# Layer-0 attention: row maxima turned by DVE in 32x32 blocks, a third bank for scores, the turned output in the bank of the values

## Chip, cores, metric

The kernel runs on 1 core of one Trainium2 chip. The metric is the device time of one execution in microseconds (us). A shorter time is better. The engines are PE (matmul), DVE (vector), ACT (scalar), POOL and SP, which here only issues DMAs.

## What is computed

Two transformer layers on x of 4 x 512 x 256 fp32, each with a modulation of its own. The change lies in the attention of layer 0, whose 16 query heads of width 16 share one key and one value head:

```python
q = x @ Wq.T                          # 16 heads of 16
kv = x @ Wkv.T
k, v = jnp.split(kv, 2, axis=-1)      # one head of 16
attn = jnp.einsum('bhqd,bkd->bhqk', q, k) / math.sqrt(HEAD_DIM)
attn = jnp.where(causal, attn, -1e9)
attn = softmax(attn, axis=-1)
out = jnp.einsum('bhqk,bkd->bhqd', attn, v)
return out.reshape(bs, seq, 256) @ Wo.T
```

Around it, `x = x + ga * attention(layernorm(x) * (1 + ca) + sa)`, and then a router with 64 experts (the best 8, an expert bias only) in the same form. Layer 1 has attention with 16 heads of 128 and a gated feed-forward part; the change doesn't touch it.

## The kernel before

The work of layer 0's attention is a loop of 44 steps for each of the 4 batches (`steps0`, written out on each engine). A batch has 4 groups (NG) of 4 heads, and a group 11 units (GU): one or more heads with a tile of 128 queries and the 512, 384, 256 or 128 keys that the causal mask leaves. Each engine runs the same steps, and at each step it does, in the order of the code, its part of several units that are at different stages. The stage of a unit is set by a lag in steps:

- **Scores**, lag 0. PE multiplies q by k (L1204, bf16 parts, 96 rows), adds the mask (L1206) into bank 0 or 1, by the parity of the step, and DVE takes the negated maximum of each row (L912, `negmax`). PE waits at step n for the reduction of step n-2 (`max0`), and at the first step of a batch for all reductions of the batch before.
- **Maxima to rows**, once a group, one group (11 steps) later. DVE splits the 16 maxima of each query into two bf16 parts (L923, L924, tile `nmp`). One step later PE turns the 128x32 tile into 32x128 (L1178, bank 4), ACT copies it (L656, tile `nmt`), and SP issues two DMAs (L429) that lay it as two rows under q in `qst`, so that the next product subtracts the maximum by itself.
- **Turned scores**, lag TURN = 17. PE multiplies k by q with the two extra rows (L1189) and adds the turned mask (L1191) into bank 2 or 3, and ACT takes the exponential into `probs` or `pT` (L664). The first unit of a group waits for the two DMAs (`nm_ready`).
- **Values**, lag VALUE = 19. At four of 11 steps PE multiplies by v (L1215) into bank 5, which holds a whole group. ACT copies it one step later (L672, `oRaw`); one step after that PE turns it (L1224) into bank 4, and DVE divides by the sums there (L930, L934, `oTok`). The next group's first values wait for the copy (`o_copied`), and the next turn of maxima for the reading of bank 4 (`oev0`).
- **After attention**, lag AFTER = 22 behind the batch: `after0(n)` spreads the output projection (n = 3 on PE, which waits for `oL` of DVE), the residual, the norm, the router, the expert bias and the next norm over 44 more steps.

SP's queue goes by a fixed order: for each group first the reload of q for the next batch (6 DMAs of 64 KB, L421, once the turned scores of the group are done), then the DMAs of maxima of a later group.

The program's order is written by hand; nothing is reordered. All engines wait on counting semaphores.

## Time and profile before

| | us |
|---|---|
| median of 3 runs | 1459.1 (1458.41 to 1460.87) |
| profiled execution, its own time | 1461.47 |
| its span, first to last instruction | 1459.7 |
| busy: PE, DVE, ACT, POOL | 1270.8, 1043.7, 678.6, 542.2 |
| mean granted clock of PE | 0.93 of full |

The busy times are of the whole span; layer 0's attention with what follows it runs from 110 us to 464 us. A time in a row of the timeline is counted from the span's start. In brackets stands how long the engine had waited before and what ended the wait. Of matmuls, a row's length includes the time in the array, so lengths of neighbours overlap, and the distance between starts is what one costs. "PEld" is PE's port for weights, which runs beside the matmuls.

### The profile page before, as it was taken

To read this page: it belongs to the slowest core of one execution; us is meant where nothing else is said; L and a number is where in the kernel's file an instruction comes from. 1 tells how busy PE (TensorE), PEld (TensorE's weight loads), DVE (VectorE), ACT (ScalarE), POOL (GpSimd) and SP (SyncE) were. 2 spreads that over 40 slices of the span, in tenths; PEclk is the share of its full clock that TensorE was granted. 3 is DMA by queue.
4 is the path that set the end of the run, shared out by engine and by line. 5 is a ranking of instruction groups with operands and counts; after the bars stand their busy time and mean duration, and the time that the engine had idled before them with its cause. 6 is when DMAs were issued, how large, how long until landed. Compare 5 with 4: busy or idle time off the path is not lost.

```text
span 1459.7 us, 25278 instructions
## 1 busy us (share of the span) xinstructions
PE 1270.8 (87%) x7740; PEld 956.4 (66%) x7740; DVE 1043.7 (71%) x3041; ACT 678.6 (46%) x1605; POOL 542.2 (37%) x496
## 2 busy tenths in 40 slices
PE   5898887776844899999899999999999899996998
PEld 3553443344443677777677778777788688785887
DVE  5766768777657876877876877876777766674773
ACT  2334534343403645545645545645655645652332
POOL 0000000000000988889888889888721300000000
PEclk8898989888856999999999999999999999998999
DMA  5121100101111010210110210110200200000000
GB/s 167 43 66 35 32 23 27 44 20 37 40 48 62 30 39 11 96 38 0 39 39 10 95 36 4 33 36 8 91 32 19 70 29 7 22 0 0 15 14 29
DMA packets 29850, 54.31 MB, mean 37 GB/s; under 512 B 5664, under 2 KB 21872, under 8 KB 29280
## 3 DMA queue, kind: packets, MB, share of 16 engines
q1 hardware_dynamic: 26544, 42.93, 8.9%
q0 software_dynamic: 2096, 6.51, 1.4%
q10 hardware_dynamic: 1152, 4.19, 0.7%
q8 instruction: 23, 0.38, 0.1%
q14 instruction: 35, 0.29, 0.1%
HBM read 41.86 MB, written 11.63 MB: 37 GB/s over the span
## 4 chain that ended last, share of the span: by engine, by line
PE 53%; DVE 34%; issue 10%; ACT 3%; DVEq 0%; DMA 0%; ACTq 0%; SPq 0%
PE bank L1307 10%; PE bank L1285 7%; PE bank L263 6%; PE bank L264 6%; PE bank L265 6%; DVE qkst L977 4%; DVE negmax L912 4%; PE bank L1296 4%; DVE qk L996 4%; PE bank L1074 3%; PE bank L1275 3%; PE bank L1204 2%; PE bank L1189 2%; PE bank L332 2%; DVE negmax L1009 1%
## 5 line engine op out<-in xcount | busy, mean ns | idle before, releaser
L528 POOL TENSOR_SCALAR gtmp<-gidx,lut 128x344 f32<-128x344 int32 (+2 forms) x210 | 301.5, 1436 | 21.3
L531 POOL TENSOR_TENSOR gacc<-gacc,gtmp 128x344 f32<-128x344 f32 (+2 forms) x210 | 183.4, 873 | 17.5
L1285 PE MATMUL bank<-kT,qT 128*128 128x128 f32 (+3 forms) x512 | 179.8, 442 | 9.2 <-ACT probs L720 9.1
L521 POOL DMA_DIRECT2D gidx<-in_idx_gate x4 | 2.2, 543 | 465.3 <-DMA h_saved<-wft 465.3
L1307 PE MATMUL bank<-pT,v 128*128 128x128 f32 x1280 | 155.4, 277 | 12.2 <-ACT pT L713 12.2
L912 DVE TENSOR_REDUCE negmax<-bank 128x1 f32<-128x512 f32 (+3 forms) x176 | 109.8, 639 | 74.3 <-PE bank L1206 73.3
L1009 DVE TENSOR_REDUCE negmax<-bank 128x1 f32<-128x128 f32 (+3 forms) x256 | 123.4, 484 | 54.6 <-PE bank L1286 53.4
L720 ACT ACTIVATE probs<-bank,negmax 128x128 f32<-128x128 f32 (+3 forms) x256 | 135.6, 530 | 49.9 <-DVE negmax L1009 47.3
L1307 PEld LDWEIGHTS bank<-pT,v 128*128 128x128 f32 x1280 | 148.0, 192 | 15.9 <-DVE oL L1019 15.9
L977 DVE BATCH_NORM_STATS2 qkst<-qk 128x6 f32<-128x128 f32 x512 | 110.0, 279 | 63.4 <-issue 63.4
L263 PE MATMUL bank<-wgH,hL 128*128 128x512 f32 x384 | 153.6, 400 | 0.1
L264 PE MATMUL bank<-wgL,hH 128*128 128x512 f32 x384 | 152.1, 396 | 0.0
L265 PE MATMUL bank<-wgH,hH 128*128 128x512 f32 x384 | 152.0, 396 | 0.0
L713 ACT ACTIVATE pT<-bank 128x128 f32<-128x128 f32 (+3 forms) x256 | 111.0, 437 | 52.0 <-PE bank L1296 51.7
L1004 DVE TENSOR_SCALAR probs<-probs,rsum 128x128 f32<-128x128 f32 (+3 forms) x256 | 123.7, 483 | 7.9
L699 ACT ACTIVATE qk<-bank 128x512 f32<-128x512 f32 x128 | 76.4, 598 | 99.5 <-PE bank L265 98.8
L1296 PE MATMUL bank<-identf,probs 128*128 128x128 f32 x640 | 112.8, 278 | 10.8 <-DVE probs L1004 7.4
L1296 PEld LDWEIGHTS bank<-identf,probs 128*128 128x128 f32 x640 | 70.0, 141 | 58.6 <-issue 28.8
L996 DVE TENSOR_TENSOR qk<-qk,sm 128x512 f32<-128x512 f32 x128 | 98.1, 835 | 0.5
L1019 DVE TENSOR_TENSOR oL<-bank,oH 128x512 fp32r<-128x512 f32 x64 | 44.1, 689 | 75.5 <-ACT oH L727 75.3
L664 ACT ACTIVATE pT<-bank 128x384 f32<-128x384 f32 (+1 forms) x112 | 58.9, 537 | 84.0 <-PE bank L1191 77.2
L1204 PE MATMUL bank<-kst,qst 96*128 96x512 bf16 (+3 forms) x256 | 73.0, 339 | 19.7 <-DVE negmax L912 18.7
(191 smaller groups left out, 2809.0 us busy)
## 6 DMA issues: line engine op xcount, KB each, us to landing
hH<-h_saved SPq DMA_DIRECT2D x16, 512.0 KB, 4.0
hL<-h_saved SPq DMA_DIRECT2D x16, 512.0 KB, 4.7
qst<-q_parts SPq DMA_DIRECT2D x96, 64.0 KB, 2.3
wg<-in_wqkv SPq DMA_DIRECT2D x4, 1536.0 KB, 8.3
wo<-in_wo SPq DMA_DIRECT2D x4, 512.0 KB, 9.2
out<-x SPq DMA_DIRECT2D x8, 256.0 KB, 2.1
x<-in_x SPq DMA_DIRECT2D x1, 1536.0 KB, 10.0
wmod<-in_wmod SPq DMA_DIRECT2D x1, 1536.0 KB, 11.9
```

Of the source, the lines that this page charges most:

```text
L263: pe.matmul(o, wL, mH, start=start, stop=False)
L264: pe.matmul(o, wH, mL, start=False, stop=False)
L265: return pe.matmul(o, wH, mH, start=False, stop=stop)
L528: link(pool.tensor_scalar(tmp if j else acc, part, float(j), lut1[0:rows, j:j + 1], ALU.is_equal, ALU.mult))
L531: link(pool.tensor_tensor(acc, acc, tmp, ALU.add))
L912: dve.tensor_reduce(negmax[:, at:at + (heads - 1) * QT + 1:QT], bank[n % 2][:, 0:heads * w].rearrange("p (h k) -> p h k", h=heads), AX.X, ...
L977: last = dve.bn_stats(qkst[:, u * HG + h, :], qk[:, u // 2, u % 2, h * HD1:(h + 1) * HD1])
L996: dve.tensor_tensor(rows, rows, r.to_broadcast([P, HG, HD1]), ALU.mult).then_inc(qk_norm, 1)
L1009: dve.tensor_reduce(negmax[:, i:i + 1], bank[SCORE_BANKS[i % 3]][:, 0:n], AX.X, ALU.max, negate=True).then_inc(max1, 1)
L1285: pe.matmul(bank[SCORE_BANKS[i % 3]][:, 0:n], qT[:, h, t * P:n], kT[:, h, 0:n], start=True, stop=False)
L1296: last = pe.transpose(bank[5 + i % 2][:, k * P:(k + 1) * P], probs[:, i % 4, k * P:(k + 1) * P], identf[:, :])
L1307: last = pe.matmul(bank[7][:, t * P:(t + 1) * P], v1[:, k, h * HD1:(h + 1) * HD1], pT1[:, h % 2, at:at + P], start=(k == 0), stop=(k == t))
```

## The change

1. The matmul that turned the maxima and ACT's copy are gone. DVE, after the split, transposes the 128x32 tile in four blocks of 32x32 (`dve.transpose`, tile `nmt` is now 128x32), after a further wait for the subtraction. Four DMAs instead of two bring it into the same two rows of `qst`, each with 32 queries of the 16 items: 2x16 pieces of 64 B, where two DMAs had 16 pieces of 256 B each. Before writing `nmt` DVE waits for the DMAs of the group before.
2. Bank 4, freed, is a third bank of scores: PE waits at step n for the reduction of step n-3 (also over the border of a batch).
3. The turned output goes into bank 5, where the values were. The next group's first values now wait for the reading of it (`oev0`).
4. TURN is 16 and not 17; VALUE and AFTER follow, 18 and 21.

```diff
-TURN = 17
+TURN = 16
+S_BANKS = (0, 1, 4)
...
-        nmt = sb(s0, "nmt", [NMP * ITEMS, P], BF16)
+        nmt = sb(s0, "nmt", [P, NMP * ITEMS], BF16)
...
-                sp.wait_ge(nm_copied, b * NG + g + 1)
-                for j in range(NMP):
-                    sp.dma_start(qst[SHIFT + j:SHIFT + j + 1, g * HG * SEQ:(g + 1) * HG * SEQ].rearrange(
-                        "p (i q) -> p i q", q=P), nmt[j * ITEMS:(j + 1) * ITEMS, :]).then_inc(nm_ready, 16)
+                sp.wait_ge(nm_turned, b * NG + g + 1)
+                rows = qst[SHIFT:ROWS0, g * HG * SEQ:(g + 1) * HG * SEQ].rearrange("p (i j q) -> p i j q", j=QT, q=VW)
+                for j in range(QT):
+                    sp.dma_start(rows[:, :, j, :], nmt[j * VW:(j + 1) * VW, :]).then_inc(nm_ready, 16)
...
-                        act.wait_ge(nm_pe, batch * NG + g + 1)
-                        if not isinstance(batch, int) or batch * NG + g > 0:
-                            act.wait_ge(nm_ready, (batch * NG + g) * NMP * 16)
-                        act.activation(nmt[:, :], bank[4][0:NMP * ITEMS, 0:P], ACT.Copy).then_inc(nm_copied, 1)
...
-                        dve.wait_ge(nm_pe, batch * NG + g)
                         nm_ch.step(dve.tensor_copy(nmp[:, 0, :], nm))
-                        dve.tensor_tensor(nmp[:, 1, :], nm, nmp[:, 0, :], ALU.subtract).then_inc(nm_split, 1)
+                        nm_ch.step(dve.tensor_tensor(nmp[:, 1, :], nm, nmp[:, 0, :], ALU.subtract))
+                        if batch * NG + g:
+                            dve.wait_ge(nm_ready, (batch * NG + g) * QT * 16)
+                        dve.transpose(nmt[:, :], nmp[:, :, :].rearrange("p j i -> p (j i)")).then_inc(nm_turned, 1)
...
-                        pe.wait_ge(nm_split, batch * NG + g + 1)
-                        if not isinstance(batch, int) or batch * NG + g > 0:
-                            pe.wait_ge(oev0, batch * NG + g - 1)
-                        pe.matmul(bank[4][0:NMP * ITEMS, 0:P], nmp[:, :, :].rearrange("p j i -> p (j i)"), identb[:, :],
-                                  start=True, stop=True).then_inc(nm_pe, 1)
...
-                            pe.wait_ge(nm_ready, (batch * NG + g + 1) * NMP * 16)
+                            pe.wait_ge(nm_ready, (batch * NG + g + 1) * QT * 16)
...
-                        pe.wait_ge(max0, b * SLOTS0 + max(n - 1, 0))
-                        to = bank[n % 2][:, 0:heads * w].rearrange("p (h k) -> p h k", h=heads)
+                        pe.wait_ge(max0, max(b * SLOTS0 + n - 2, 0))
+                        to = bank[S_BANKS[(b * SLOTS0 + n) % 3]][:, 0:heads * w].rearrange("p (h k) -> p h k", h=heads)
...
-                            pe.wait_ge(o_copied, batch * NG + g)
+                            pe.wait_ge(oev0, batch * NG + g)
...
-                            last = pe.transpose(bank[4][:, t * P:(t + 1) * P], oRaw[:, t * P:(t + 1) * P], identf[:, :])
+                            last = pe.transpose(bank[5][:, t * P:(t + 1) * P], oRaw[:, t * P:(t + 1) * P], identf[:, :])
```

How PE's order moves, in the group whose scores are of heads 12 to 15 in batch 0. From the last scores of the group before (4 heads x 128 keys) to the first step of this one, before:

```order
L1204 MATMUL bank0<-kst,qst 128x128 [waits max0]
L1204 MATMUL bank0<-kst,qst 128x128 x3
L1206 MATMUL bank0<-maskb,identb 128x512
L1189 MATMUL bank2<-qst,kst 128x384 [waits exp0]
L1191 MATMUL bank2<-maskT,identb 128x128
L1204 MATMUL bank1<-kst,qst 128x512 [waits max0,q_loaded3]
L1206 MATMUL bank1<-maskb,identb 128x128
L1215 MATMUL bank5<-probs,vS 32x512 [waits exp0,o_copied]
L1215 MATMUL bank5<-probs,vS 32x512 x3
L1178 MATMUL bank4<-identb,nmp 32x128 [waits o0_ready,negmax_split]
L1189 MATMUL bank3<-qst,kst 128x384 [waits exp0]
```

And now (L1192, L1194, L1177, L1179 and L1203 are the lines that were L1204, L1206, L1189, L1191 and L1215):

```order
L1192 MATMUL bank4<-kst,qst 128x128 [waits max0]
L1192 MATMUL bank4<-kst,qst 128x128 x3
L1194 MATMUL bank4<-maskb,identb 128x512
L1203 MATMUL bank5<-probs,vS 32x512 [waits exp0,o0_ready]
L1203 MATMUL bank5<-probs,vS 32x512 x3
L1177 MATMUL bank3<-qst,kst 128x384 [waits exp0]
L1179 MATMUL bank3<-maskT,identb 128x128
L1192 MATMUL bank0<-kst,qst 128x512 [waits max0,q_loaded3]
L1194 MATMUL bank0<-maskb,identb 128x128
L1177 MATMUL bank2<-qst,kst 128x384 [waits exp0]
```

The values now stand ahead of the group's first score and wait for `o0_ready`; L1178 with its two waits is gone. Further on in the same group, the place where PE waits for the DMAs of maxima, now:

```order
L1177 MATMUL bank3<-qst,kst 128x512 [waits exp0]
L1179 MATMUL bank3<-maskT,identb 128x512
L1192 MATMUL bank1<-kst,qst 128x384 [waits max0]
L1194 MATMUL bank1<-maskb,identb 128x128
L1177 MATMUL bank2<-qst,kst 128x512 [waits exp0,negmax_ready]
L1179 MATMUL bank2<-maskT,identb 128x128
L1192 MATMUL bank4<-kst,qst 128x384 [waits max0]
```

The matmul with `negmax_ready` was one step later before: a score of 384 keys stood between it and the L1192 above it. On DVE, where a group's maxima are split, now:

```order
L906 TENSOR_REDUCE negmax<-bank4 128x1 [waits scores0]
L916 CAST nmp<-negmax 128x16 [waits max0]
L917 TENSOR_TENSOR nmp<-negmax,nmp 128x16 [waits dve_chain4]
L920 STREAM_TRANSPOSE nmt<-nmp 128x32 [waits dve_chain4]
L906 TENSOR_REDUCE negmax<-bank0 128x1 [waits scores0]
```

L920 is new, with its wait for the subtraction (and, from the second group on, one for the DMAs before).

## Rows read from the trace of the kernel before

**Rows 1.** the page's part 4, the chain that ended last: share by engine
```profile
PE 53%; DVE 34%; issue 10%; ACT 3%; DVEq 0%; DMA 0%; ACTq 0%; SPq 0%
```

**Rows 2.** windows: stretch, length, busy time and count of each engine, granted clock, DMA
```profile
110.16:174.00 63.84, 58.20 (x423) 25.65 (x424) 44.70 (x88) 31.80 (x60) 0.00 (x0) 0.89 0.14 37
174.00:380.00 206.00, 156.20 (x1083) 87.70 (x1082) 153.66 (x413) 78.09 (x169) 0.00 (x0) 0.85 0.08 27
```

**Rows 3.** waits from 257.3 to 339.1: waiting, releaser: total us, times, longest
```profile
DVE negmax L912 <- PE bank L1206: 18.2, 10, 5.2
PEld bank L1178 <- DVE nmp L924: 8.5, 3, 4.2
```

**Rows 4.** timeline of DVE, batch from 257 us: start, length, work, [wait before, releaser]
```profile
268.00 0.56 DVE L912 TENSOR_REDUCE negmax<-bank 128x1 f32<-128x384 f32 x1 [5.21 <-PE bank L1206]
...
282.79 0.69 DVE L912 TENSOR_REDUCE negmax<-bank 128x1 f32<-128x512 f32 x1 [0.85 <-PE bank L1206]
...
289.11 1.06 DVE L912 TENSOR_REDUCE negmax<-bank 128x1 f32<-128x384 f32 x2 [2.17 <-PE bank L1206]
...
295.52 0.69 DVE L912 TENSOR_REDUCE negmax<-bank 128x2 f32<-128x512 f32 x1 [3.70 <-PE bank L1206]
...
299.61 0.69 DVE L912 TENSOR_REDUCE negmax<-bank 128x1 f32<-128x512 f32 x1 [0.62 <-PE bank L1206]
...
301.58 0.69 DVE L912 TENSOR_REDUCE negmax<-bank 128x1 f32<-128x512 f32 x1 [0.47 <-PE bank L1206]
...
321.93 0.69 DVE L912 TENSOR_REDUCE negmax<-bank 128x1 f32<-128x512 f32 x1 [0.54 <-PE bank L1206]
```

**Rows 5.** timeline of PE, 150 to 163 us
```profile
150.30 0.38 PE L1204 MATMUL bank<-kst,qst 96*128 96x512 bf16 x1 [0.65 <-DVE negmax L912]
150.52 0.22 PE L1206 MATMUL bank<-maskb,identb 128*128 128x128 bf16 x1
...
151.81 0.23 PE L1178 MATMUL bank<-identb,nmp 128*32 128x128 bf16 x1
151.97 0.34 PE L1189 MATMUL bank<-qst,kst 98*128 98x384 bf16 x1
...
152.20 0.38 PE L1204 MATMUL bank<-kst,qst 96*128 96x512 bf16 x1
...
155.59 0.33 PE L1204 MATMUL bank<-kst,qst 96*128 96x384 bf16 x1
...
155.81 0.38 PE L1189 MATMUL bank<-qst,kst 98*128 98x512 bf16 x1
...
162.55 0.23 PE L1178 MATMUL bank<-identb,nmp 128*32 128x128 bf16 x1 [0.17 <-DVE nmp L924]
```

**Rows 6.** two small DVE operations, all their executions: ns min/median/max
```profile
L924 DVE TENSOR_TENSOR nmp<-negmax,nmp x16: 174/175/177, 119.1 to 381.1; 128x16 bf16<-128x16 f32 x16
L930 DVE RECIPROCAL rsum_t<-bank x16: 243/252/258, 138.1 to 405.2; 128x16 f32<-128x16 f32 x16
```

**Rows 7.** the transfers of the maxima, L429: ns of one issue, and landing
```profile
L429 SPq DMA_DIRECT2D qst<-nmt x32: 502/582/607, 119.9 to 382.4; - x32
...
DMA to landing us min/median/max: 1.7/1.8/2.4
```

**Rows 8.** timeline of DVE, the split of the group at 151 us
```profile
151.58 0.17 DVE L924 TENSOR_TENSOR nmp<-negmax,nmp 128x16 bf16<-128x16 f32 x1
```

**Rows 9.** timeline of PE, the turn of the maxima in the batch from 257 us
```profile
281.39 0.29 PE L1178 MATMUL bank<-identb,nmp 128*32 128x128 bf16 x1 [2.47 <-DVE nmp L924]
```

**Rows 10.** the product that writes oTok, all its executions
```profile
L934 DVE TENSOR_TENSOR oTok<-bank,rsum_t x16: 423/424/426, 138.3 to 405.5; 128x256 f32<-128x256 f32 x16
```

**Rows 11.** windows of the granted clock, columns as in rows 2
```profile
281.40:287.30 5.90, 5.90 (x25) 2.31 (x25) 4.69 (x8) 2.44 (x5) 0.00 (x0) 0.50 0.01 1
302.80:306.10 3.30, 1.49 (x13) 0.28 (x11) 3.13 (x11) 0.74 (x2) 0.00 (x0) 1.00 0.01 1
```

**Rows 12.** timeline of SP's queue, one reload of q
```profile
144.47 2.73 SPq L421 DMA_DIRECT2D qst<-q_parts  x6
```

More of the change, by code:

```diff
@@ L649, in steps0 @@
                 for n in range(SLOTS0):
-                    i, batch = at_step(n, GU + 1, b, scores, values)
-                    if i is not None and i % GU == 0:
-                        g = i // GU
-                        act.wait_ge(nm_pe, batch * NG + g + 1)
-                        if not isinstance(batch, int) or batch * NG + g > 0:
-                            act.wait_ge(nm_ready, (batch * NG + g) * NMP * 16)
-                        act.activation(nmt[:, :], bank[4][0:NMP * ITEMS, 0:P], ACT.Copy).then_inc(nm_copied, 1)
                     i, batch = at_step(n, TURN, b, scores, values)
@@ L912, in steps0 @@
                         dve.tensor_reduce(negmax[:, at:at + (heads - 1) * QT + 1:QT],
-                                          bank[n % 2][:, 0:heads * w].rearrange("p (h k) -> p h k", h=heads),
+                                          bank[S_BANKS[(b * SLOTS0 + n) % 3]][:, 0:heads * w].rearrange("p (h k) -> p h k", h=heads),
                                           AX.X, ALU.max, negate=True).then_inc(max0, 1)
@@ L928, in steps0 @@
                         dve.wait_ge(o_turned, batch * NG + g + 1)
-                        pv = bank[4][:, :].rearrange("p (t h d) -> p t h d", t=QT, d=VW)
+                        pv = bank[5][:, :].rearrange("p (t h d) -> p t h d", t=QT, d=VW)
                         dve.reciprocal(rsum0_t[:, :, :, :], pv[:, :, :, HD0:HD0 + 1]).then_inc(rsum0, 1)
@@ L1171, in steps0 @@
                 for n in range(SLOTS0):
-                    i, batch = at_step(n, GU + 1, b, scores, values)
-                    if i is not None and i % GU == 0:
-                        g = i // GU
-                        pe.wait_ge(nm_split, batch * NG + g + 1)
-                        if not isinstance(batch, int) or batch * NG + g > 0:
-                            pe.wait_ge(oev0, batch * NG + g - 1)
-                        pe.matmul(bank[4][0:NMP * ITEMS, 0:P], nmp[:, :, :].rearrange("p j i -> p (j i)"), identb[:, :],
-                                  start=True, stop=True).then_inc(nm_pe, 1)
                     i, batch = at_step(n, TURN, b, scores, values)
```

8 lines of the change are left out of this document (4 added, 4 removed).

## Prediction

> **What bounds the kernel now.** I read the chain that ended last first: PE and DVE share it, with hardly any DMA on it [rows 1]. The change touches layer 0's attention alone, so next I cut that stage out with the table of windows: 64 us of it (110 to 174) have only attention on the engines, and PE is busy for 58 of them; the next 206 us also carry the work behind attention (output projection, router, two norms), and there neither engine is full, PE 156 us and DVE 154 us [rows 2]. So the first stretch is bound by PE and the second by the hand-over between PE and DVE. The list of waits of one whole batch, 257.3 to 339.1, says what hands over late: DVE waited ten times, 18.2 us in all, for scores, and PE's weight port three times, 8.5 us in all, for the split maxima [rows 3]. The timeline of DVE has those ten waits one by one; six stand in [rows 4]. The longest, 5.21 us, lies behind the output projection: PE's order puts the projection behind one more unit of scores, and PE can't start the projection before DVE has written oL. A third bank doesn't move a score ahead of that. The 3.70 us behind the router's logits are of this kind too. What the change can reach are the short ones.
>
> **The change part by part.** In steps of the loop: scores of unit n at step n, turned scores at n-16 (was n-17), values and everything after them one step earlier likewise. A group has 11 steps.
>
> *Turn of the maxima on PE and its copy on ACT, removed.* 16 matmuls; the start-to-start time from L1178 at 151.81 to L1189 at 151.97 is 0.16 us [rows 5], and PE waited 0.17 us for the split before the one at 162.55. In the PE-bound stretch both are gained. The ACT copy was beside other work, and I cost it at nothing.
>
> *32x32 transpose on DVE, added.* It comes after a second wait within the chain. No row shows this operation. Below, it is about the 0.175 us of the small subtraction, above, the 0.25 us of the reciprocal of 16 elements [rows 6]; I take 0.2 us, since it too is bound by its start and not by its 32 elements, and 0.25 us with the wait that makes the subtraction end first. (The Trainium skill, "VectorE: DVE Perf Modes", section "The three transpose paths", gives 311 ns for 128 columns of bf16; by that it would be 0.3 us here and the sum some 0.5 us longer.) It counts only where DVE is on the path.
>
> *Four transfers of 2x16 pieces of 64 B, instead of two of 16 pieces of 256 B.* SP issues them one after the other, 0.58 us each, and the last lands 1.8 us after its issue [rows 7]. Two: 0.58 + 1.8 = 2.4 us. Four: 3 x 0.58 + 1.8 = 3.5 us. And the consumer now stands one step nearer. Take the group at 151. The last score ahead of the split is L1206 at 150.52; the subtraction starts at 151.58 and takes 0.17 us [rows 5, 8]. Now: 151.75 + 0.2 + 0.05 for SP to wake + 3.5 = the rows are in place at 155.5. PE, for its part, would reach the first turned scores of the group like this: the old way from 151.97 to 155.81 is 3.84 us; one step less takes off one turned score of 384 columns (151.97 to 152.20, 0.23 us) and one score (155.59 to 155.81, 0.22 us) [rows 5], so 3.4 us, counted now from 150.6, since values and maxima's turn no longer stand between. PE is there at 154.0 and waits 1.5 us. Queued behind this wait stand, in PE's order, the score of the same step, two pieces of values, and all that follows; DVE runs dry meanwhile, and nobody else has work for PE. A group of the PE-bound stretch then costs 10.74 (151.81 to 162.55 [rows 5]) - 0.16 - 0.17 + 1.5 = 11.9 us, 1.2 more. Four groups are in that position (the turned scores at steps 27, 38, 49, 60): +4.8 us. In the second stretch the same 3.5 us is covered: 206 us over 110 steps [rows 2] are 1.87 us a step, and five steps 9.4 us.
>
> *Third bank for scores.* PE may be two reductions ahead rather than one, and the rule at a batch's first step (all reductions of the batch before) goes. That frees 0.65 us of PE at 150.30 [rows 5]. In the batch from 257, of the DVE waits of [rows 4] go 0.85, 0.62, 0.47 and 0.54 us, 2.5 us; the first and the last came because PE stood before L1178, 2.47 us at 281.39 [rows 9], and then started late. Against it 4 x 0.25 us of transposes: 1.5 us gained a batch. Two batches run so whole, of a third only the 0.85 us less 0.5 us of transposes: 3.35 us gained.
>
> *Turned output in the bank of the values.* Values of the next group now wait for oTok to be read, not just for the copy. By the order below, two whole steps of PE (1.2 us) lie between the turn and those values, and DVE needs 0.25 + 0.42 us for reciprocal and product [rows 6, 10]: hidden, if DVE isn't behind; where it is behind, it has two reductions in hand while PE does the 1.1 us of values. I cost it at nothing; without that cover it would be 0.7 us a group.
>
> *Tail.* Without scores the chain is DVE's, so the last transpose costs its 0.25 us.
>
> **Sum**, against the profiled execution (1461.5 us): first stretch +4.8 - 0.65 = +4.15; second -3.35; tail +0.25: **+1.0 us**. The median of the runs shown, 1459.1, is 2.4 us below the profiled one; I carry the difference over: **1460.0 us**. What a measurement of this kernel can tell from no change is about 0.2%, 2.9 us.
>
> **Rivals.**
> (a) *PE's clock drops at the new wait: slower.* In the four fast groups PE would stand 1.5 us in every 12. For it: after 2.47 us of standing before L1178 the next 5.9 us were granted 0.50, 1.2 GHz [rows 9, 11]. Against it: from 302.80 to 306.10 PE was busy only 1.49 of 3.30 us and kept 1.00, 2.4 GHz [rows 11]. If it drops, a stretch of 4 to 6 us at half clock costs 2 to 3 us, four times: +8 to 12 us, 1470. It decides where the wait is nearer 2.5 than 1.5 us.
> (b) *The wait is short and PE stays warm: faster.* SP issued the six loads of q in 2.73 us, 0.46 us each [rows 12]; at that pace and a landing of 1.7 us the four transfers take 3.1 us and PE waits 1.1 us, -1.6 us over four groups. And where PE no longer stands before L1178 the stretch from 281.4 is perhaps not at half clock: its 2.17 us wait of DVE [rows 4] then shrinks by up to 1.5 us a batch, -3 to -4 us. Together 1455. Against it: PE will then just stand for the norm instead, as DVE is the slower one from 268 to 286.
> (c) *The small pieces land late: slower.* The slowest landing of the old ones was 2.4 us [rows 7]; with twice the pieces for each transfer, at a quarter of the size, 0.6 to 1 us more on every group's wait, 4 to 5 groups: 1463 to 1465. The Trainium skill, "DMA: Bandwidth & Descriptors", section "Specifications", speaks for this (under 512 B the DMA engine reads, changes and writes back); by that rule the late landing would show in every transfer. The old pieces of 256 B are under it already and landed in 1.8 us.
> (d) That the change doesn't do what it says: the third bank is real only if PE gets two scores ahead, and PE's waits for oL, hN and hL bring it back to one. That is in the sum, where those waits of DVE stay.
>
> **How the numbers follow.** My forecast, gain and loss cancel: 0.38. (a) 0.17, (b) 0.30, (c) 0.15. Faster by over 0.2%: most of (b) and an edge of the forecast, 0.29. Within 0.2%: 0.37. Slower by over 0.2%: (a), (c) and the other edge, 0.34. The range goes from below (b), with all of the short DVE waits gone, 1453, to (a) at its middle, 1469.
>
> **What would show it.** The turned score's first matmul should be listed as waiting on a DMA at four places between 122 and 170, 1.5 us each; L1178's waits gone; the list of DVE's waits for scores near 15.7 us a batch, with the 5.21 and 3.70 us unchanged; the transposes at 0.2 us; the transfers' landing at 1.8 us. The stretch up to the first output projection should be 4 us longer and each later batch 1.5 us shorter. I am wrong if the batches shrink by 3 us or more, if no wait for the transfers shows, or if the granted clock between 125 and 174 falls below 1.00.

## The result and the profile after

| | us |
|---|---|
| before, median of all its runs beside the changed kernel | 1460.65 (1458.35 to 1468.21, 20 runs) |
| after, median | 1465.62 (1459.31 to 1470.88, 20 runs) |
| ratio after : before | 1.0029, 95% interval 1.0015 to 1.0043 |
| profiled execution of after | 1469.84, span 1468.0 |

The change makes the kernel slower by 0.29%, some 4 to 5 us, where I forecast no change. The executions of one kernel lie up to 12 us apart: of before's 20, 13 took 1458.4 to 1460.9 us and seven 1462.5 to 1468.2 us; of after's 20, seven took 1459.3 to 1462.7 us and 13 took 1465.2 to 1470.9 us. The profiled execution of after is one of the latter and lies 4.2 us above the median, so the lengths below, which are of that execution, overstate the loss, and no trace shows an execution of the seven.

The chain that ended last looks as before, with DMA and SP's queue now on it at 1% each, where [rows 1] has 0%:

```profile
PE 50%; DVE 36%; issue 10%; ACT 3%; DMA 1%; SPq 1%; DVEq 0%; ACTq 0%
```

To see where the time went, I cut both spans at the same events: the first score of layer 0, the first operation of the work behind attention (L826 before, L820 after) in each of three batches, and the first statistics of layer 1. The windows of before, columns as in [rows 2]: the first stretch, two whole batches, the rest of layer 0, layer 1.

```profile
110.16:173.87 63.71, 58.07 (x422) 25.52 (x423) 44.57 (x88) 31.80 (x60) 0.00 (x0) 0.89 0.14 37
173.87:254.97 81.10, 61.65 (x435) 34.06 (x436) 61.65 (x170) 30.86 (x66) 0.00 (x0) 0.87 0.07 21
254.97:336.71 81.74, 61.80 (x431) 33.86 (x430) 61.75 (x170) 31.32 (x67) 0.00 (x0) 0.85 0.11 33
336.71:467.12 130.41, 75.71 (x448) 49.35 (x447) 89.20 (x262) 39.09 (x90) 0.00 (x0) 0.70 0.13 47
467.12:1459.70 992.58, 926.87 (x5715) 760.63 (x5713) 716.37 (x2162) 509.23 (x1240) 539.32 (x483) 0.99 0.09 32
```

The same windows of after:

```profile
108.34:179.13 70.79, 58.33 (x414) 26.51 (x414) 43.83 (x90) 30.72 (x55) 0.00 (x0) 0.88 0.12 33
179.13:263.58 84.45, 65.35 (x433) 35.61 (x430) 62.47 (x175) 29.81 (x62) 0.00 (x0) 0.84 0.07 20
263.58:345.28 81.70, 65.33 (x428) 34.99 (x427) 62.28 (x175) 30.08 (x63) 0.00 (x0) 0.79 0.10 33
345.28:474.94 129.66, 74.79 (x448) 48.83 (x447) 90.38 (x269) 38.13 (x86) 0.00 (x0) 0.71 0.12 47
474.94:1468.00 993.06, 926.86 (x5716) 760.97 (x5715) 717.03 (x2162) 508.87 (x1240) 539.77 (x483) 0.99 0.09 32
```

The first stretch is 7.1 us longer, the first whole batch 3.4 us; the second is level, the rest of layer 0 is 0.7 us shorter, and layer 1 is the same to 0.5 us. In the first stretch PE is busy for the same 58 us, at nearly the same clock; what was added is idle time. In the two batches it is the reverse: PE is busy for 65.3 us instead of 61.7 with the same work, at a granted clock of 0.84 and 0.79 instead of 0.87 and 0.85.

What PE waits for in the first stretch, before (waiting, releaser: total us, times, longest):

```profile
PE bank L1204 <- DVE negmax L912: 2.4, 7, 0.7
PE bank L1178 <- DVE nmp L924: 1.5, 3, 1.1
```

And after:

```profile
PE bank L1177 <- DMA qst<-nmt: 9.9, 5, 2.9
PE bank L1192 <- DVE negmax L906: 1.5, 5, 0.7
```

The wait for the transfers is the forecast's main term. It is there five times (2.90, 1.71, 1.80, 1.77 and 1.76 us). The timeline of PE has the first, the third and the fourth of them, with the next turned score of 512 columns behind the latter two (start, length, work, wait before):

```profile
120.08 0.61 PE L1177 MATMUL bank<-qst,kst 98*128 98x512 bf16 x1 [2.90 <-DMA qst<-nmt]
...
144.92 0.39 PE L1177 MATMUL bank<-qst,kst 98*128 98x512 bf16 x1 [1.80 <-DMA qst<-nmt]
...
146.35 0.61 PE L1177 MATMUL bank<-qst,kst 98*128 98x512 bf16 x1
...
158.41 0.39 PE L1177 MATMUL bank<-qst,kst 98*128 98x512 bf16 x1 [1.77 <-DMA qst<-nmt]
...
159.67 0.61 PE L1177 MATMUL bank<-qst,kst 98*128 98x512 bf16 x1
```

The same instruction takes 0.39 us right behind the wait and 0.61 us 1.3 us later. The windows of the granted clock say why, the stretch ahead of the wait first:

```profile
142.00:144.92 2.92, 1.12 (x12) 0.32 (x5) 1.46 (x3) 0.60 (x1) 0.00 (x0) 1.00 0.06 8
...
146.35:148.95 2.60, 2.60 (x21) 1.09 (x18) 0.56 (x1) 0.78 (x2) 0.00 (x0) 0.50 0.27 77
...
159.67:162.69 3.02, 3.02 (x21) 1.24 (x18) 0.74 (x2) 1.20 (x3) 0.00 (x0) 0.50 0.28 86
```

PE stood for 1.80 us and kept 2.4 GHz through it; then, fully busy again, it ran at 1.2 GHz for 2.6 us and more; the fall lies 0.9 us behind the wait. Behind the fourth and the fifth wait it fell likewise, 1.0 and 1.4 us on. Behind the second wait (1.71 us, at 132.63) it did not fall. At the first wait, from 117.18 to 120.08, it fell while PE still stood. The last part of that wait:

```profile
118.50:120.08 1.58, 0.00 (x0) 0.00 (x0) 0.00 (x0) 0.00 (x0) 0.00 (x0) 0.50 0.03 3
```

The kernel before runs at half clock nearly as long in this stretch (14 us against 17), but at another place: once, early, where PE is mostly busy and no wait is longer than 1.13 us, and not again. Its windows, the second up to the end of the stretch:

```profile
113.24:126.89 13.65, 11.74 (x47) 4.77 (x48) 9.69 (x18) 3.41 (x6) 0.00 (x0) 0.50 0.10 19
126.89:173.87 46.98, 44.32 (x367) 20.14 (x366) 32.35 (x67) 28.39 (x55) 0.00 (x0) 1.00 0.13 35
```

So the half clock behind the new waits is real, and yet it is hardly a part of the 7.1 us between the two kernels here, since in after the early half clock comes only with the first wait and is half as long: the mean clock is 0.88 against 0.89. In the two batches behind it is otherwise, as the busy times above show.

The transfers and the transposes, all their executions; then one group on SP's queue and on DVE:

```profile
L431 SPq DMA_DIRECT2D qst<-nmt x64: 596/610/807, 116.2 to 391.0; - x64
L920 DVE STREAM_TRANSPOSE nmt<-nmp x16: 211/211/213, 116.0 to 388.8; 128x32 bf16<-128x32 bf16 x16
```

```profile
154.67 2.61 SPq L431 DMA_DIRECT2D qst<-nmt  x4
```

```profile
154.43 0.21 DVE L920 STREAM_TRANSPOSE nmt<-nmp 128x32 bf16<-128x32 bf16 x1
```

SP begins 0.03 us after the transpose ends, and PE is released 3.74 us later, at 158.41. The forecast had 0.05 and 3.5 us.

In the batch from 263.58, DVE's waits for scores (first row: all of them in this batch) and the four longest:

```profile
DVE negmax L906 <- PE bank L1194: 17.6, 9, 5.2
```

```profile
276.95 0.69 DVE L906 TENSOR_REDUCE negmax<-bank 128x1 f32<-128x512 f32 x1 [5.04 <-PE bank L1194]
...
296.56 1.06 DVE L906 TENSOR_REDUCE negmax<-bank 128x1 f32<-128x384 f32 x2 [1.24 <-PE bank L1194]
...
302.28 0.56 DVE L906 TENSOR_REDUCE negmax<-bank 128x1 f32<-128x384 f32 x1 [3.01 <-PE bank L1194]
...
319.97 0.56 DVE L906 TENSOR_REDUCE negmax<-bank 128x1 f32<-128x384 f32 x1 [5.24 <-PE bank L1194]
```

Against [rows 3, 4]: 5.21, 2.17 and 3.70 us are 5.04, 1.24 and 3.01 now, and the short waits of 0.85, 0.62, 0.47 and 0.54 us don't stand there. But one of 2.54 us in before has become 5.24 us, so that the sum is 17.6 instead of 18.2 us. PE's waits between 174 and 420 us show what happened to its idle time. Before:

```profile
PE bank L1204 <- DVE negmax L912: 16.4, 23, 1.1
PE bank L263 <- DVE oL L833: 15.1, 4, 3.9
PE bank L1178 <- DVE nmp L924: 13.9, 5, 3.3
PE bank L332 <- DVE hN L313: 7.1, 3, 4.9
```

After:

```profile
PE bank L264 <- DVE oL L827: 15.9, 3, 5.5
PE bank L333 <- DVE hN L314: 10.7, 5, 4.5
PE bank L1192 <- DVE negmax L906: 8.5, 15, 1.2
PE bank L387 <- DVE ex L862: 6.6, 3, 2.7
PE bank L1203 <- DVE oTok L930: 6.0, 6, 1.7
```

PE runs ahead further, no longer stops for the split, stops half as long for maxima, and then stands longer where it needs the work behind attention: up to 5.5 us instead of 3.9 us for oL.

### The profile page after: what moved, and what is told of

Its sections match the earlier page's. It is cut to its first block, busy times and chain, and to the rows that moved or that the text cites. A ratio compares the mean times of both kernels' runs of the same rounds, so it can differ in the third digit from the quotient of the medians.

```text
span 1468.0 us, 25248 instructions
## 1 busy us (share of the span) xinstructions
PE 1276.5 (87%) x7724; PEld 960.2 (65%) x7724; DVE 1046.1 (71%) x3057; ACT 673.9 (46%) x1589; POOL 542.7 (37%) x496
## 4 chain that ended last, share of the span: by engine, by line
PE 50%; DVE 36%; issue 10%; ACT 3%; DMA 1%; SPq 1%; DVEq 0%; ACTq 0%
PE bank L1295 10%; PE bank L1273 7%; PE bank L264 5%; PE bank L265 5%; PE bank L266 5%; DVE qk L992 4%; DVE qkst L973 4%; DVE negmax L906 4%; PE bank L1284 4%; PE bank L1070 3%; PE bank L1263 2%; PE bank L333 2%; DVE negmax L1005 1%; PE bank L1177 1%; DVE hN L310 1%
## 5 line engine op out<-in xcount | busy, mean ns | idle before, releaser
L906 DVE TENSOR_REDUCE negmax<-bank 128x1 f32<-128x512 f32 (+3 forms) x176 | 109.5, 637 | 81.3 <-PE bank L1194 80.4
L264 PE MATMUL bank<-wgH,hL 128*128 128x512 f32 x384 | 153.7, 400 | 0.1
L266 PE MATMUL bank<-wgH,hH 128*128 128x512 f32 x384 | 152.3, 397 | 0.0
L1000 DVE TENSOR_SCALAR probs<-probs,rsum 128x128 f32<-128x128 f32 (+3 forms) x256 | 123.3, 482 | 7.9
L1273 PEld LDWEIGHTS bank<-kT,qT 128*128 128x128 f32 x512 | 77.5, 191 | 17.5 <-ACT probs L714 15.2
```

The source lines that it names most:

```text
L264: pe.matmul(o, wL, mH, start=start, stop=False)
L266: return pe.matmul(o, wH, mH, start=False, stop=stop)
L906: dve.tensor_reduce(negmax[:, at:at + (heads - 1) * QT + 1:QT], bank[S_BANKS[(b * SLOTS0 + n) % 3]][:, 0:heads * w].rearrange("p (h k) -> ...
L1273: pe.matmul(bank[SCORE_BANKS[i % 3]][:, 0:n], qT[:, h, t * P:n], kT[:, h, 0:n], start=True, stop=False)
```

## The experiments

Three theories stood at the start. T1: the transfers' wait and the half clock that follows it are the loss. T2: the third bank gathers PE's idle time into long stops and is the loss. T3: the transposes on DVE. The table has all runs. "Layer 0" is the stretch from the first score to the first statistics of layer 1, "layer 1" what is behind it, both of the one profiled execution; the last column has the median of all executions. Lengths without a fence are taken from windows cut like the ones above.

| kernel | first stretch | three parts of layer 0 behind it | layer 0 | layer 1 | median (ratio to before, 95%) |
|---|---|---|---|---|---|
| before | 63.7 | 81.1, 81.7, 130.4 | 357.0 | 992.6 | |
| e8 before again | 63.7 | 80.6, 82.1, 130.6 | 357.0 | 992.4 | 1459.2, one run |
| after | 70.8 | 84.5, 81.7, 129.7 | 366.6 | 993.1 | 1465.6 (1.0015 to 1.0043) |
| e1 n-17 | 62.1 | 79.7, 82.0, 128.9 | 352.6 | 990.1 | 1456.6 (0.9939 to 0.9976) |
| e2 two banks | 68.4 | 81.4, 81.1, 131.6 | 362.6 | 990.6 | 1461.3 (0.9977 to 1.0009) |
| e3 transposes alone | 63.8 | 82.5, 81.6, 129.8 | 357.7 | 984.9 | 1454.0 (0.9943 to 0.9977) |
| e4 two on ACT's queue | 79.3 | 87.4, then 223.0 | 389.7 | 990.7 | 1492.1 (1.0186 to 1.0230) |
| e5 e3 + shared bank | 65.0 | 83.7, 81.2, 129.9 | 359.8 | 985.9 | 1454.1 (0.9937 to 0.9971) |
| e6 two on POOL's queue | 63.1 | 80.5, 79.8, 129.7 | 353.1 | 993.6 | 1457.8 (0.9959 to 0.9995) |
| e7 matmuls added | 65.4 | 79.8, 81.1, 129.8 | 356.1 | 993.0 | 1459.2 (0.9972 to 1.0011) |
| e9 e7 + before L387 | 65.4 | 79.8, 81.1, 130.0 | 356.3 | 986.1 | 1455.2 (0.9951 to 0.9979) |
| e10 e5 + before L264 | 63.6 | 82.1, 82.2, 125.3 | 353.2 | 985.6 | 1450.8 (0.9909 to 0.9950) |
| e11 e1 + POOL's queue | 60.2 | 82.9, 80.4, 128.9 | 352.4 | 993.9 | 1454.6 (0.9928 to 0.9969) |
| e12 e7, two banks | 68.0 | 81.5, 81.2, 131.6 | 362.3 | 990.4 | 1460.7 (0.9980 to 1.0015) |

Layer 1, whose code is the same in all, differs by up to 9 us, and the start ahead of the first score, the same code too, by up to 4 us (106.9 us in e3, 111.2 us in e5). The totals carry both. Each kernel but before was traced in one execution, while its executions are up to 12 us apart (e7, 1452.7 to 1465.0 us). Which part of a kernel that spread comes from is not known, so a column and a median need not tell the same.

### e8: the kernel before once more

> The kernel before once more, for a second profile. Two stretches that the change doesn't touch differ between the profiles so far: the start up to the first score (110.2 us before, 106.9 to 109.0 in the others) and all that follows layer 0 (992.6 us before, 984.9 to 993.1 in the others). If these are chance, this profile differs from the first by as much in them; if they come with the change, it repeats 110.2 and 992.6 within 0.5 us. The first stretch of attention should repeat its 63.7 us within 1 us either way.

Measured: the first stretch is repeated to 0.01 us, layer 0 to 0.1 us and layer 1 to 0.2 us; only the start up to the first score, 107.9 us instead of 110.2, is chance. Of the whole, the stretches of layer 0 are the part to judge the change by, with the reserve that two executions of one kernel, both of its quicker ones, are little to know their scatter by. Layer 1 is repeated as well, and yet its code is not the change's: the last section has what moves with it.

### e1: one step more for the transfers

```diff
-TURN = 16
+TURN = 17
```

> The changed kernel with its turned scores at step n-17 again (values, turn of the output and output projection follow, each one step later); transposes, four transfers, third bank and shared bank stay. PE then reaches the first turned scores of a group one step later, about 1 us in the stretch bound by PE. Theory T1 (the wait for the transfers, and the half clock that follows it, are the loss): the wait of 1.7 to 1.8 us at the first turned scores shrinks to 0.7 to 0.9 us, PE keeps 1.00 behind it, first stretch 68 us or less instead of 70.8, time 2 to 4 us below the changed kernel. Theory T2 (the loss lies in the batches behind, where the third bank turns many short stops of PE into few long ones): transfer waits shrink too, but the time stays within 1.5 us of the changed kernel, since batches from 179 on keep their 84.5 and 81.7 us. Theory T3 (the transposes on DVE are the loss): no change.

Measured: 1456.6 us, 9 us below after. The waits for transfers in the first stretch fall from 9.9 us to 3.2 us, of which 2.3 us is the first group's:

```profile
PE bank L1177 <- DMA qst<-nmt: 3.2, 4, 2.3
```

The first stretch is 8.7 us shorter than after's, more than the 6.7 us of waits, and PE is busy for 55.0 us in it instead of 58.3, at a clock of 0.95 instead of 0.88. T1 stands; T3 falls, since the transposes are all still there. The size was beyond the range that I had given T1; in the profiles layer 0 is 14.0 us shorter and layer 1, which the edit doesn't touch, 3.0 us.

### e2: two banks for scores

```diff
-                        pe.wait_ge(max0, max(b * SLOTS0 + n - 2, 0))
-                        to = bank[S_BANKS[(b * SLOTS0 + n) % 3]][:, 0:heads * w].rearrange("p (h k) -> p h k", h=heads)
+                        pe.wait_ge(max0, b * SLOTS0 + max(n - 1, 0))
+                        to = bank[n % 2][:, 0:heads * w].rearrange("p (h k) -> p h k", h=heads)
```

> The changed kernel with two PSUM banks for scores in place of three; all else stays. T1: the third bank is a gain that the transfer waits hide, so without it the time is 3 us above the changed kernel, DVE's short waits for scores (0.85, 0.62, 0.47, 0.54 us) are back. T2: the third bank gives nothing or costs: the time is 0 to 2 us below the changed kernel, the wait of 5.24 us of DVE behind L387 is short again (2.5 us) and the expert bias on PE takes 1.9 us instead of 3.8. T3: as T1, since the transposes stay: 3 us above.

Measured: 1461.3 us, 4.3 us below after: at n-16 the third bank costs. The place is the one that T1 names. With two banks PE arrives later at the first turned scores, so it waits less there:

```profile
PE bank L1177 <- DMA qst<-nmt: 6.6, 5, 2.1
```

So neither theory had it as it is: the third bank lengthens the transfers' wait, 3.3 us of it in the first stretch. Behind e2's four later waits, of 1.08 to 1.17 us, the clock did not fall.

### e3 and e5: the transposes alone, and with the shared bank

e3 undoes the third bank, the shared bank and the shift of the step; what is left of the change is the transpose on DVE and the four transfers. The turned output is back in bank 4:

```diff
-TURN = 16
+TURN = 17
...
-                            pe.wait_ge(oev0, batch * NG + g)
+                            pe.wait_ge(o_copied, batch * NG + g)
...
+                        pe.wait_ge(oev0, batch * NG + i // GU)
                         for t in range(QT):
-                            last = pe.transpose(bank[5][:, t * P:(t + 1) * P], oRaw[:, t * P:(t + 1) * P], identf[:, :])
+                            last = pe.transpose(bank[4][:, t * P:(t + 1) * P], oRaw[:, t * P:(t + 1) * P], identf[:, :])
```

> Of the change only the transposes on DVE with their four transfers: turned scores at step n-17, two banks for scores, the turned output in the bank that the turned maxima had. Against the kernel before, T1: PE saves 0.16 and 0.17 us a group, the four transfers are 1.1 us longer, the wait of PE at the first turned scores is 0.7 us or less in the stretch bound by PE: time within 2 us of the kernel before. T2: the same, within 2 us. T3: the transposes and their waits cost DVE 0.25 us at 16 groups, and up to 0.5 us with what queues behind: 4 us above the kernel before.

e5 is e2 with `TURN = 17`.

> As e3 (transposes on DVE, turned scores at n-17, two banks for scores) and the turned output in the bank of the values; or as e1 without the third bank. By the profiles of e1 and e3 the third bank takes 1.7 us off the first stretch and 2.8 and 1.9 us off two of the batches at n-17. If sharing the bank costs nothing, this kernel comes out like e3, 1454 us. If sharing costs what the third bank gives (e1 stands at 1456.6, e3 at 1454.0), it is 5 us or more above e3, near 1460, and DVE or PE shows a wait at the first values of a group (L1203 on oTok) that e3 has not.

Measured: 1454.0 and 1454.1 us. Layer 0 takes 357.7 us in e3, before's 357.0 within 1 us, as T1 and T2 both said; the median lies 6.6 us below before's, and what is shorter in the profile is code that the edit doesn't touch: layer 1 (984.9 against 992.6 us) and the start (106.9 against 110.2 us). The transposes and the four transfers, set against the matmul and the copy that they replace, thus cost next to nothing at n-17. Sharing the bank costs nothing in the medians. In the profiles e5's layer 0 is 2.1 us longer than e3's, but PE waited for the bank only once between 174 and 420 us, for 0.4 us.

### e4 and e6: two of the four transfers on another queue

e4 has ACT issue the third and fourth transfer, at step n-11; in e6 it is POOL, with a semaphore of its own:

```diff
-                for j in range(QT):
+                for j in range(QT // 2):
...
+            for b in range(NB):
+                for g in range(NG):
+                    pool.wait_ge(nm_turned, b * NG + g + 1)
...
+                    for j in range(QT // 2, QT):
+                        pool.dma_start(rows[:, :, j, :], nmt[j * VW:(j + 1) * VW, :]).then_inc(nm_ready2, 16)
```

> The changed kernel with the third and fourth transfer of each group issued by ACT instead of SP. The last transfer then starts after one issue of 0.6 us instead of three, about 1.2 us earlier, if ACT is free; ACT pays two issues, 1.2 us a group, between exponentials. T1: the waits of 1.7 to 1.8 us at the first turned scores fall to 0.5 to 0.7 us and the half clock behind 144.9 and 158.4 is gone: first stretch 3 to 6 us shorter, time 3 us below the changed kernel, unless ACT's exponentials are delayed by its 1.2 us (then PE waits for exponentials instead, and it gives back up to that, 4 groups of 1.2 us). T2: first stretch shorter, but the batches behind unchanged or longer: time within 1.5 us. T3: no change.

> The changed kernel (n-16, three banks) with the third and fourth transfer of each group issued by POOL, which has no work in this stage, each queue with a semaphore of its own. SP's part then starts one issue of 0.6 us after the first, about 1.2 us earlier than the fourth does now. T1 (the transfers' wait and the half clock behind it cost some 8 us in the first stretch): waits of PE for transfers fall from 11.3 us in 7 places to 3 to 5 us, the first stretch from 70.8 to 64 to 66 us, time 1458 to 1461. If POOL's queue lands later than SP's by more than 1.2 us, waits stay or grow: time at 1466 or above. T2: time within 1.5 us of 1465.6.

e4 is a miss of my making: 1492.1 us. ACT waits for the transposes with the exponentials of older groups queued behind that wait, and PE then waits for ACT, in the first stretch:

```profile
PE bank L1184 <- ACT pT L665: 11.6, 5, 2.8
```

The transfers' wait did go but for one of 2.3 us; the loss, which I had bounded by ACT's 1.2 us of issuing, is ACT's wait. The trace has the place: ACT reaches its issues ahead of the transposes and stands there in each of the 16 groups, with the issues 95.4 us in all, while an exponential waits behind them (at 160.03 us it had waited 4.24 us, with the transposes at 158.36). e6 has no such queue behind it, and is 7.8 us below after, 1457.8. Issue to landing on POOL's queue takes 1.8 us (the page's part on DMA issues), and the waits are halved:

```profile
PE bank L1186 <- DMA qst<-nmt: 5.2, 5, 1.9
```

```profile
qst<-nmt POOLq DMA_DIRECT2D x32, 2.0 KB, 1.8
```

4.7 us of waits less, and a first stretch 7.7 us shorter, with PE busy for 54.4 us instead of 58.3 and a clock of 0.95. As in e1, PE's speed comes back with the waits: 2.0 us beside 6.7 us of waits there, 3.0 us beside 4.7 us here. In both, the half clock at the first wait is still there, and the three falls behind the later waits are gone. Those waits are 0.73 to 1.00 us in e6.

### e7, e9 and e12: matmuls that only keep the clock

e7 is after with seven matmuls added ahead of the wait, whose results nobody reads:

```diff
                         if i % GU == 0:
+                            if b <= 1 and n < 22 or b == 0:
+                                for _ in range(7):
+                                    pe.matmul(bank[6][:, 0:4 * P], identb[:, :], kst[:, 0:SEQ], start=True, stop=True)
                             pe.wait_ge(nm_ready, (batch * NG + g + 1) * QT * 16)
```

> The changed kernel with work added: seven matmuls of 512 columns into an idle bank ahead of PE's wait for the transfers, at the five groups of the first stretch. They take 7 x 0.22 = 1.5 us at full clock and nobody reads them. If half the loss is the half clock that follows the wait (146.35 to 148.95 and 159.67 to 162.69 at half speed), PE stays at 1.00 behind 144.9 and 158.4, and the first stretch is 2 to 4 us shorter than 70.8: 1462 to 1463. If the clock isn't decided by the wait, the stretch stays or grows by up to 0.5 us at each of five places, to 73 us, and the time is 1466 to 1468.

Measured: 1459.2 us, 6.4 us below after, with 1.5 us of work added at five places. The transfers land as late as before; PE still stands, or computes for nobody, until they do. But its clock in the first stretch is 0.97, and the first stretch is 5.4 us shorter:

```profile
110.70:176.13 65.43, 59.91 (x449) 27.68 (x449) 44.06 (x90) 30.50 (x55) 0.00 (x0) 0.97 0.13 36
```

Of its 59.9 us, 7.7 us are the 35 added matmuls, so the work itself took 52.2 us instead of 58.3. That is what full clock is worth in this stretch, measured alone, and it is more than what after lost against before, whose own 58.1 us hold the early half clock: the granted clock was 0.50 for some 17 us of the stretch in after, 14 us in before and 3 us in e7. The three falls behind the later waits are worth 3.3 to 3.9 us of it, by PE's busy time in e1 and e6.

e9 adds eight more matmuls ahead of L387, in each batch:

```diff
+                    for _ in range(8):
+                        pe.matmul(bank[7][:, 0:4 * P], identb[:, :], kst[:, 0:SEQ], start=True, stop=True)
                     pe.wait_ge(r_w, b + 1)
```

> e7 (seven added matmuls ahead of the transfers' wait) and eight more of 512 columns ahead of L387's wait for the router's weights, in each batch; 8 x 0.22 = 1.8 us inside a stop of 2.6 to 2.7 us. The stop stays, the half clock behind it (L1158 at 3.78 us instead of 1.92) should go. If the third bank's gain is given back by the half clock behind this longer stop, the wait of 5.24 us of DVE at 320 falls to about 3.4, and each of the three batches is 1 to 2 us shorter than in e7 (79.8, 81.1, 69.0): time 1455 to 1457. If what gives it back is PE's order (whatever PE's speed, DVE waits for the scores behind that stop), the batches keep e7's lengths within 0.5 us: 1459.

The batches keep e7's lengths to 0.1 us. In e7 the clock behind this stop was full to begin with, though the stop is as long as after's. L387 and the expert's bias behind it, in after:

```profile
228.37 0.29 PE L387 MATMUL bank<-identb 128*128 128x128 bf16 x1 [2.67 <-DVE ex L862]
...
232.70 3.78 PE L1158 MATMUL bank<-ebias,wT 64*128 64x256 f32 x8
```

And in e7:

```profile
224.79 0.23 PE L387 MATMUL bank<-identb 128*128 128x128 bf16 x1 [2.67 <-DVE ex L862]
...
227.11 1.99 PE L1158 MATMUL bank<-ebias,wT 64*128 64x256 f32 x8
```

The same stop of 2.67 us, once with half speed behind it and once without. So this stop does not decide by itself. The same place one batch later has DVE's wait of 5.24 us behind it. In after and e1 the stop is 2.67 and 2.59 us, the product (L1158 in most) takes 3.78 us and DVE waits 5.24 us; in e6 and e7, with three banks too, the stop is 2.66 and 2.67 us, the product takes 1.99 us and DVE waits 2.54 us; in before and e2, with two, it is 1.07 and 1.02 us, with 1.99 and 2.54 us behind it. The third bank thus lengthens the stop, and the 5.24 us are the half clock's. What decides whether the clock falls there, I can't say. The median of e9, 1455.2, is 4 us below e7's, and in the profiles that is layer 1 (986.1 against 993.0 us).

e12 is e7 with e2's edit, two banks.

> e7 (n-16, seven added matmuls ahead of the transfers' wait) with two banks for scores in place of three. e7 stands at 1459.2 us; its three batches are 79.8, 81.1 and 69.0 us. If the third bank is worth what the prediction gave it once PE's clock holds (0.65 us in the first stretch, 1.5 us a batch), this kernel is 3 to 4 us slower, 1462 to 1463, its DVE waits for scores in the second batch near 18 us instead of 16.6. If the third bank is worth nothing, because what DVE doesn't wait for at its short waits it waits for at the next long one, the batches are within 0.5 us of e7's and the time is 1458 to 1460. If it costs, as e2 against the changed kernel (1461.3 against 1465.6) and e5 against e1 (1454.1 against 1456.6) say, it is 1455 to 1457.

Layer 0 takes 362.3 us, 6.2 us more than in e7: 2.6, 1.7, 0.1 and 1.8 us by its four parts. The medians are 1.5 us apart, 1460.7 and 1459.2, with intervals that overlap. At n-17 the profiles say the same (e5 less e1: 7.1 us), while the medians there, 1454.1 and 1456.6, say the reverse. Most of both gains is PE's clock and not the hand-over that the bank was meant for: in the first two parts PE is busy for 63.4 and 63.7 us in e12 against 59.9 and 61.3 us in e7, and for 59.2 and 65.2 us in e5 against 55.0 and 61.1 us in e1. Only the rest of layer 0 is shorter with three banks in all three pairs, by 1.9 us (after against e2), 1.8 us (e7 against e12) and 1.0 us (e1 against e5). So layer 0 is shorter with the third bank in two pairs of single profiles; why, beyond those 1 to 2 us, and what it is worth in the whole time stay open.

### e10 and e11: what could still be had

e10 is e5 with the same remedy at PE's longest stop, fourteen matmuls into bank 4, idle there:

```diff
+                    for _ in range(14):
+                        pe.matmul(bank[4][:, 0:4 * P], identb[:, :], kst[:, 0:SEQ], start=True, stop=True)
                     pe.wait_ge(ot_lo, (b + 1) * KT)
```

> e5 (turned scores at n-17, two banks, shared bank) with fourteen added matmuls of 512 columns, 3.1 us, into the bank that is idle there, ahead of the output projection's wait for oL, where PE stands 3.7 to 3.9 us and was granted 0.50 for the 5 us behind it (265 to 270). The projection's matmuls take 0.58 us each at half clock; at full clock they take half. If the clock holds, the projection ends 2 to 2.5 us earlier in each of four batches, DVE's longest wait (5 us) shrinks by it, 6 to 9 us in all: 1446 to 1449. If DVE, at 4.8 of 5.0 us busy ahead of it and behind it, takes the place of PE as the bound, half of it: 1450 to 1451. If the added matmuls don't hold the clock: 1454 to 1456.

Measured: 1450.8 us, the fastest of all, 0.7% below before (ratio 0.993, interval 0.9909 to 0.9950, which overlaps e5's 0.9937 to 0.9971). By the profiles 3.8 us of it are layer 0 (353.2 us against 357.0) and 7.0 us layer 1, whose short length it shares with e5. The projection runs at full clock in e10: the matmuls of L266 in it take 0.42 us in the median in e5 and at most 0.28 us in e10. First e5, then e10, each over the 5 us that hold its beginning:

```profile
265.00:270.00 5.00, 2.89 (x13) 2.90 (x14) 2.61 (x5) 0.00 (x0) 0.00 (x0) 0.50 0.00 0
```

```profile
260.00:265.00 5.00, 4.31 (x29) 3.10 (x28) 3.07 (x5) 0.00 (x0) 0.00 (x0) 1.00 0.00 0
```

Layer 0 is 6.6 us shorter than e5's, as expected in sum, but not where I expected it: 1.4, 1.6, -1.0 and 4.6 us in its four parts. The first of these holds no projection, so its 1.4 us are not the edit's. In the second whole batch the granted clock was 0.83, in e5 0.87, with the added matmuls in it: what was kept behind L264 was lost elsewhere.

e11 is e1 with e6's edit.

> e1 (turned scores at n-17, three banks, shared bank) with POOL's queue for two of the four transfers. Of e1's waits for transfers in the first stretch, 3.2 us, all but some 1 us should go. If a wait for transfers was still e1's loss, the first stretch falls from 62.1 to about 60 us and the time from 1456.6 to 1454 to 1455. If the third bank only moves PE's idle time from many short stops to few long ones (T2), the batches behind keep e1's 79.7, 82.0 and 68.1 us, and the time stays within 1 us of 1456.6.

1454.6 us, and the first stretch 60.2 us, as expected: one wait of 1.3 us is left there. The batches came out at 82.9 and 80.4 us against e1's 79.7 and 82.0; their sum moved by 1.6 us, which decides nothing on T2.

## Why the prediction was right or wrong

1460.0 us was forecast and 1465.6 measured, inside the range of 1453 to 1469. Against before's median beside it, the forecast's +1.0 us was +5.0 us. The forecast proper, that gain and loss cancel, did not come true; slower by over 0.2% had 0.34, drawn mostly from rivals (a) and (c), of which (c) did not come true. In the first stretch the terms as measured add up without the clock: the forecast's 4.15 us, 1.8 us for a fifth wait and some 1.0 us for four waits of 1.71 to 1.80 us instead of 1.5 make 6.95 us, where 7.1 us were measured. In the first whole batch 3.4 us were lost, and PE was busy for 3.7 us longer there, at a granted clock of 0.84 instead of 0.87. One of the signs of being wrong showed: the granted clock fell below 1.00 between 125 and 174. Point by point:

- **The turn on PE, removed; the transpose.** Right: 0.211 us for 0.2, and L1178's waits gone.
- **Four transfers, "PE is there at 154.0 and waits 1.5 us"**: the mechanism was right and the sizes too small. First issue to release took 3.74 us, not 3.5 us, as one issue takes 0.61 us, not 0.58, and the first of a group up to 0.81. The place of PE was read from before, where it has two banks; with a third it is further ahead when the last maxima come. So 1.71 to 1.80 us at four places (e2 has 6.6 us in place of 9.9).
- **"Four groups are in that position"**: it was five; this was the largest mistake of the first stretch. The turned scores at step 16 wait too, 2.90 us. In before PE stood 1.13 us for the split there, so this place alone cost some 1.8 us that the sum lacked.
- **Rival (a), the clock, at 0.17**: the forecast left the clock out of its sum, and that is the other step that failed. I let it decide at a wait "nearer 2.5 than 1.5 us". It fell at 2.90 us and behind 1.80, 1.77 and 1.76 us, not behind 1.71 us, and at 2.67 us in one kernel and not in another. [rows 11] had a stretch of PE half idle at full clock, which I took as the rule; it was one case. Rival (a) had "4 to 6 us at half clock", four times, 8 to 12 us; the falls behind the later waits last some 3 us each and cost 3.3 to 3.9 us together, and in the first stretch they are offset by an early half clock that before has and after has only half as long. That this offset exists is luck; neither the sum nor the rival had it.
- **Rival (b), short waits and a warm PE**: no. The four issues took 2.61 us and not 4 x 0.46, and the waits were 1.7 to 2.9 us and not 1.1 us. DVE's wait of 2.17 us did shrink, to 1.24 us, but the batch was no shorter.
- **Third bank, "1.5 us gained a batch"**: in the batch from 263.58 the short waits that the forecast named don't stand where they stood, though others of 0.83, 0.40 and 0.21 us do; 17.6 us are left where 15.7 us were forecast, and with 1.0 us for four transposes the batch came out level (81.70 against 81.74). The first whole batch came out 3.4 us longer. With the transfers' wait filled, e7 against before has -1.3, -0.6 and -0.7 us, 2.6 us in all, against the forecast 3.35. That is near, but e12 shows that most of it is not the short waits' doing, so it doesn't confirm the term. In after it was not to be had.
- **Shared bank at nothing**: right with two banks (0.4 us of waiting). With three, PE waits 6.0 us for oTok between 174 and 420 us; it arrives earlier at each place, and these waits stand where others would.
- **Rival (c), late small pieces**: no. The four issues take 2.61 us, so the last begins 2.0 us behind the first, and PE is released 1.7 us after that; POOL's landed in 1.8 us, as before's did [rows 7]. The rule of the Trainium skill, "DMA: Bandwidth & Descriptors", section "Specifications", on pieces under 512 B shows no price here between pieces of 256 B and of 64 B.
- **Rival (d)**: the third bank is real, and its lead is taken back at L264 and L333, as the rival had it, and at L387 (DVE's ex), which it did not name.

## What to carry to other kernels

Where a transfer replaces a path over an engine, count issue by issue on its queue, and set it against the consumer's place in the kernel after, not before: here one step of lead (1 us of PE's work) was worth 9 us, and the third bank alone lengthened each wait by some 0.7 us. A wait of PE in a stretch that it bounds can cost more than its length, because its clock may fall at it or behind it (at four of five waits here); if the wait can't be removed, fill it. Before a half clock is put down to a new wait, though, look whether the kernel before has one of its own: by PE's busy time the two were equal here. And an edit that lets an engine run ahead (the third bank) should be tried again after the wait at its front is gone: the same edit cost 4 us of layer 0 at n-16 with that wait and gained 6 to 7 us of layer 0 in single profiles of two kernels where it is short or filled, though no median shows the gain.

## What the runs showed of the hardware that I had not expected

PE's clock can fall after the stop, while PE is fully busy: 1.00 through the 2.92 us with the wait, 0.50 from 0.9 us behind it. It can also fall in the stop: at 118.5, 1.6 us ahead of the end of the wait of 2.90 us, and at 227.7, 0.7 us ahead of the end of the one of 2.67 us. And the same stop does it or doesn't: 1.80 us yes and 1.71 us no in one kernel, 2.67 us yes and no in two. The Trainium skill, "TensorE: Matmul & The Clock Gate", section "HAM oscillation — how this bites in real kernels", tells of a matmul loop whose clock is lost at every wait for a DMA; here it was lost at four of five. The same page, section "What's actually happening", has the chip's monitor running freely, not in step with the kernel. The traces fit that: the fall comes at no fixed distance from a stop. That it also comes in a stretch in which PE was busy for 58 of 64 to 71 us I had not drawn from it.

In the 14 traces layer 1 takes one of a few lengths: 984.9 to 986.1 us (e3, e5, e9, e10), 990.1 to 990.7 (e1, e2, e4, e12) or 992.4 to 993.9 (before twice, after, e6, e7, e11). The code is the same, and e7 and e9 differ by eight matmuls a batch in layer 0. The part that moves is DVE's beside POOL's work: the product of L1004 in before, then the same in e9 (L1000), between 500 and 900 us (busy, mean ns of one, idle before):

```profile
L1004 DVE TENSOR_SCALAR probs<-probs,rsum 128x512 f32<-128x512 f32 (+1 forms) x121 | 63.1, 521 | 3.7
```

```profile
L1000 DVE TENSOR_SCALAR probs<-probs,rsum 128x512 f32<-128x512 f32 (+1 forms) x121 | 60.7, 501 | 3.7
```

In the profiles with the short layer 1 this product takes 491 to 501 ns, in the others 511 ns (e4) to 521 ns, and DVE is busy in layer 1 for 709 to 712 us instead of 716 to 718. It doesn't tell the middle length from the long one: e1 has 520 ns at 990.1 us. The Trainium skill, "SBUF — State Buffer", section "SBUF: two separate sides", has one pair of ports that POOL and DVE, in some of its modes, share as a lock, held by whichever starts first. By that, if this product runs in such a mode, the phase between the two engines' streams, set anywhere before, could decide how often it waits. No run here tried it; it is open, and so is whether the length goes with the kernel or changes from one execution to the next. It is as large as the whole effect of the change, so that the 0.4% by which e1, e3 and e5 lie below before need not be their own; in e3's profile nothing of it is layer 0's.
